# Gates of a query block applied tile by tile, and the gate bias as a fifth entry beside the experts' logits, in a two-layer graph and attention network on one core

## The reference: what is computed

```python
sx = jnp.einsum('bsh,ndh->bnsd', x, hl_w) + hl_b[None, :, None, :]
pad = sx == 0
q = jnp.einsum('bnsd,neod->bneso', sx, wq)
k = jnp.einsum('bnsd,nod->bnso', sx, wk)
v = jnp.einsum('bnsd,nod->bnso', sx, wv)
scores = jnp.einsum('bnesd,bntd->bnest', q, k) * d ** 0.5 + causal
att = jax.nn.softmax(scores, axis=-1)
qkv = jnp.einsum('bnest,bntd->bnesd', att, v)
qkv = jnp.where(pad[:, :, None], 0.0, qkv)
out = jnp.transpose(qkv, (0, 1, 3, 2, 4)).reshape(b, nh, s, ne * d)
gs = jax.nn.softmax(jnp.einsum('bnsf,nef->bnse', out, gate_w) + gate_b[None, :, None, :], axis=-1)
mixed = jnp.einsum('bnsed,bnse->bnsd', out.reshape(b, nh, s, ne, d), gs)
hn = layernorm(mixed + resid, ln_g, ln_b)
```

## Time and profile before

| | |
|---|---|
| median of 3 runs | 3369.95 us (3368.48 to 3369.95) |
| the profiled execution | 3364.28 us, span 3362.6 us |
| granted clock of TensorE, mean | 0.934 |
| PE matmuls | 2953.1 us busy, 88% |
| POOL | 1772.2 us, 53% |
| DVE | 1898.3 us, 56% |
| ACT | 1254.0 us, 37% |
| PE's row maxima L1736, held by DVE's reading L1906 | 91.4 us in 52 waits |

### The profile page before, as it was taken

The page is one execution under the profiler, slowest core; times in us unless marked ns, Lnnn a source line. Parts: engine busy times, 40 slices in busy tenths (PEclk is TensorE's granted clock), DMA queues, the critical chain, the costliest instruction groups (busy, mean ns, idle before and its releaser), DMA issues. The chain is left out here.

```text
span 3362.6 us, 45520 instructions
## 1 busy us (share of the span) xinstructions
PE 2953.1 (88%) x17338; PEld 1822.7 (54%) x17338; DVE 1898.3 (56%) x3632; ACT 1254.0 (37%) x1712; POOL 1772.2 (53%) x956
## 2 busy tenths in 40 slices
PE   7998987679997889899999999788988999999953
PEld 3467666468885455555555555455555554545532
DVE  3555764487733465665655651245656565565566
ACT  2232320355633233343434344323433443434433
POOL 0030020233220357778889899636687888888014
PEclk9999888889998899999999999888999999999976
DMA  9961100299970000000000000000000000000001
GB/s 391 423 246 41 63 1 8 87 290 282 268 130 18 1 1 1 1 1 1 1 1 1 1 4 1 1 1 1 1 1 1 1 1 1 1 1 1 1 8 36
DMA packets 63624, 195.20 MB, mean 58 GB/s; under 512 B 8244, under 2 KB 25010, under 8 KB 53427
## 3 DMA queue, kind: packets, MB, share of 16 engines
q1 hardware_dynamic: 38658, 147.98, 11.4%
q0 software_dynamic: 24752, 44.31, 7.3%
HBM read 188.86 MB, written 3.41 MB: 57 GB/s over the span
## 5 line engine op out<-in xcount | busy, mean ns | idle before, releaser
L2052 POOL TENSOR_TENSOR at_acc<-at_acc,at_pt 128x1024 f32<-128x1024 f32 (+3 forms) x674 | 1445.8, 2145 | 257.4 <-ACT at_pt L1843 178.0
L1843 ACT ACTIVATE at_pt<-at_psR 128x1024 f32<-128x1024 f32 (+3 forms) x776 | 697.8, 942 | 993.2 <-PE at_psR L1752 686.7
L1906 DVE TENSOR_REDUCE at_mx<-at_psR 128x2 f32<-128x1024 f32 x576 | 702.1, 1225 | 493.5 <-PE at_psR L1736 492.0
L1770 PE MATMUL at_psO<-at_pt,v 128*64 128x512 f32 (+3 forms) x3104 | 716.5, 584 | 2.1 <-DVE at_oT L1939 1.8
L1736 PE MATMUL at_psR<-at_khi,at_qhi 64*128 64x512 f32 (+3 forms) x1568 | 353.5, 447 | 134.4 <-DVE at_mx L1906 91.4
L1736 PEld LDWEIGHTS at_psR<-at_khi,at_qhi 64*128 64x128 f32 x1568 | 155.8, 189 | 411.8 <-issue 360.2
L1770 PEld LDWEIGHTS at_psO<-at_pt,v 128*64 128x64 f32 x3104 | 194.2, 140 | 339.6 <-issue 239.1
L1316 PE MATMUL ga_acc<-h,ga_ring 128*128 128x257 f32 (+1 forms) x1352 | 304.7, 385 | 31.0 <-ACT ga_ring L1210 27.3
L1749 PE MATMUL at_psR<-at_qhi,at_klo 64*128 64x512 f32 (+2 forms) x1552 | 307.8, 392 | 6.6 <-ACT at_pt L1843 5.7
L1316 PEld LDWEIGHTS ga_acc<-h,ga_ring 128*128 128x128 f32 (+1 forms) x1352 | 257.3, 192 | 76.6 <-ACT ga_ring L1210 36.0
L1749 PE MATMUL at_psR<-at_qlo,at_khi 64*128 64x512 f32 (+2 forms) x1552 | 294.7, 375 | 0.0
(11 more groups left out here) (335 smaller groups left out, 3531.3 us busy)
## 6 DMA issues: line engine op xcount, KB each, us to landing
gc_rows<-in_adj SPq DMA_DIRECT2D x26, 1664.0 KB, 17.4
ga_rows<-in_adj SPq DMA_DIRECT2D x26, 1664.0 KB, 9.9
ga_ring<-in_adjT POOLq DMA_DIRECT2D x78, 512.0 KB, 23.6
gc_cols<-in_adjT SPq DMA_DIRECT2D x26, 1024.0 KB, 14.9
gc_ring<-in_adjT SPq DMA_DIRECT2D x26, 512.0 KB, 8.2
gc_ring<-in_adjT SPq DMA_DIRECT2D x13, 256.0 KB, 2.8
ga_ring<-in_adjT POOLq DMA_DIRECT2D x13, 256.0 KB, 11.0
out_x<-X SPq DMA_DIRECT2D x6, 512.0 KB
```

The lines of the kernel that those rows point to most:

```text
L1770: ins = pe.matmul(columns(psO[lanes[l], :], g), v1[:, t, (2 * hp + l) * D:(2 * hp + l + 1) * D], packed(pt[:, g % PTS, l, 0:w], g), start= ...
L1843: act.activation(pt[:, g % PTS, :, 0:w], psR[:, slot_of["score", g] % SLOTS, :, 0:w], ACT.Exp).then_inc(e_ready, 1)
L1906: dve.tensor_reduce(mx[:, u % 2, :, s, c:c + 1].rearrange("p l o -> p (l o)"), got[:, :, 0:w], AX.X, ALU.max).then_inc(p1_read, 1)
L2052: pool.tensor_tensor(to, to, got, ALU.add).then_inc(added, 1)
```

## The change

`gate_pieces` keeps pieces 0 and 1 in their steps. Piece 2 is gone from it. In its place POOL weighs one tile of 128 queries per instruction (`weigh`), tiles 0 and 1 behind its adds of step 3, tiles 2 and 3 behind those of step 4. DVE sums the experts of one tile at a time (`sum_of_experts`) between the first and the second maxima of a step: in steps 5, 6, 7 and 8 counted from the start of unit e = 0 (in block 3 the last two are steps 0 and 1 of unit e = 1; in block 2 the steps are 4, then two tiles in step 0 and one in step 1 of unit e = 1). The tile's statistics follow behind the step's second maxima. Where a unit has fewer than five steps, all tiles are weighed, summed and measured in the step in which the pieces stood. ACT waits by tiles. The reduce writes into `scrap`, which the maxima's instructions use too, in place of `mixed`.

The gate bias is no longer added. `onx` has a fifth entry: ACT writes the biases of the half's two heads there (`gate_biases`, once per half), POOL writes ones as its denominators, and the reciprocal, the product and the sum of piece 0 run over five entries.

```diff
@@ -1534,12 +1534,38 @@
     if u and e == 0:
         hp, b, _ = UNITS[u - 1]
         if ls >= 5:
-            return [(hp, b, i) for i in range(3) if k == 2 + i]
-        return [(hp, b, i) for i in range(3 if ls == 1 else 1)] if k == ls - 1 else []
+            return [(hp, b, i) for i in range(2) if k == 2 + i]
+        return [(hp, b, i) for i in range(2 if ls == 1 else 1)] if k == ls - 1 else []
     if u > 1 and e == 1 and steps_of(u) == 3 and k == 0:
         hp, b, _ = UNITS[u - 2]
-        return [(hp, b, 1), (hp, b, 2)]
+        return [(hp, b, 1)]
     return []
+
+
+def block_weighed(u, k):
+
+    ls, e = steps_of(u), UNITS[u][2]
+    if u and e == 0:
+        hp, b, _ = UNITS[u - 1]
+        if ls >= 5:
+            return [(hp, b, s) for s in range(SUB) if k == 3 + s // 2]
+        return [(hp, b, s) for s in range(SUB)] if ls == 1 else []
+    if u > 1 and e == 1 and steps_of(u) == 3 and k == 0:
+        hp, b, _ = UNITS[u - 2]
+        return [(hp, b, s) for s in range(QBLOCKS[b][1] // P)]
+    return []
+
+
+SUM_STEPS = {5: (4, 5, 5, 6), 7: (5, 6, 7, 8)}
+
+
+def block_summed(u, k):
+
+    ls, e = steps_of(u), UNITS[u][2]
+    if not u or ls < 5 or e > 1:
+        return block_weighed(u, k)
+    hp, b, _ = UNITS[u - 1 - e]
+    return [(hp, b, s) for s in range(SUB) if SUM_STEPS.get(ls, (5, 6, 7, 8))[s] == k + e * ls]
 
 
 FIRST_TURNS = [("k", 0, 0), ("q", 0), ("q", 1), ("r", 0), ("k", 0, 1), ("q", 2)]
@@ -1606,20 +1632,19 @@
...
-        junk = m.sb("at_junk", [P, P])
+        scrap = m.sb("at_scrap", [P, P])
...
-        onx = m.sb("at_onx", [P, SUB, NE, 2 * NE + 2])
-        rden = m.sb("at_rden", [P, SUB, NE, 2])
-        gp = m.sb("at_gp", [P, SUB, NE, 2 * NE])
+        onx = m.sb("at_onx", [P, SUB, NE + 1, 2 * NE + 2])
+        rden = m.sb("at_rden", [P, SUB, NE + 1, 2])
+        gp = m.sb("at_gp", [P, SUB, NE + 1, 2 * NE])
...
-        mixed = m.sb("at_mixed", [P, SUB, P])
...
@@ -1826,7 +1855,9 @@
...
-                        act.wait_ge(mix_done, block_number(hp, b))
+                        last = block_number(hp, b) - 1
+                        seen = min(s0 + 2, QBLOCKS[last % NQB][1] // P) if EXPERTS[b] == 1 else SUB
+                        act.wait_ge(mix_done, tiles_upto(last // NQB, last % NQB) + seen)
...
@@ -1848,9 +1879,18 @@
...
+                        if b == NQB - 1 and hp + 1 < NPR:
+                            gate_biases(hp + 1)
+
+                def gate_biases(hp):
+                    both = gb_sb[:, 2 * hp:2 * hp + 2, :].rearrange("p l g -> p (l g)")
+                    act.activation(onx[:, :, NE, 0:2 * NE], both.unsqueeze(1).broadcast_to([P, SUB, 2 * NE]),
+                                   ACT.Copy).then_inc(bias_set, 1)
...
+                act.wait_ge(w_loaded, 64)
+                gate_biases(0)
...
@@ -1963,47 +2005,55 @@
...
+                        dve.wait_ge(bias_set, hp + 1)
...
-                                [P, ws * NE, 2, NE]), ALU.mult))
+                                [P, ws * (NE + 1), 2, NE]), ALU.mult))
...
-                        link(dve.tensor_tensor(gl[:, 0:ws, :], gl[:, 0:ws, :],
-                                               gb_sb[:, 2 * hp:2 * hp + 2, :].rearrange("p l g -> p (l g)").unsqueeze(
-                                                   1).broadcast_to([P, ws, 2 * NE]), ALU.add))
...
-                    elif piece == 1:
+                    else:
...
-                                          rden[:, 0:ws, :, :], ALU.mult).then_inc(gate_ready, 1)
-                    else:
-                        dve.wait_ge(weighed, at_block + 1)
-                        if at_block < NPR * NQB - 1:
-                            link(dve.tensor_reduce(mixed[:, 0:ws, :], on[:, 0:ws, :, :].rearrange("p s e c -> p s c e"),
-                                                   AX.X, ALU.add))
-                        else:
-                            link(dve.tensor_tensor(on[:, 0:ws, 0:2, :], on[:, 0:ws, 0:2, :], on[:, 0:ws, 2:4, :], ALU.add))
-                            link(dve.tensor_tensor(mixed[:, 0:ws, :], on[:, 0:ws, 0, :], on[:, 0:ws, 1, :], ALU.add))
-                        hsl = hn[:, c0 // P:c0 // P + ws, hp * P:(hp + 1) * P]
-                        dve.tensor_tensor(hsl, hsl, mixed[:, 0:ws, :], ALU.add).then_inc(mix_done, 1)
-                        dve.wait_ge(mix_done, at_block + 1)
-                        for s in range(ws):
-                            for l in range(2):
-                                ins = dve.bn_stats(hn_stats[:, s, l, :], hsl[:, s, l * D:(l + 1) * D])
-                        link(ins)
-                        for s in range(ws):
-                            for l in range(2):
-                                ins = dve.bn_aggr(hn_mv[:, c0 // P + s, 2 * hp + l, :], hn_stats[:, s, l, :])
-                        link(ins)
+                                          rden[:, 0:ws, 0:NE, :], ALU.mult).then_inc(gate_ready, 1)
+
+                def statistics(hp, tile, s):
+                    for l in range(2):
+                        ins = dve.bn_stats(hn_stats[:, s, l, :], hn[:, tile, hp * P + l * D:hp * P + (l + 1) * D])
+                    link(ins)
+                    for l in range(2):
+                        ins = dve.bn_aggr(hn_mv[:, tile, 2 * hp + l, :], hn_stats[:, s, l, :])
+                    return ins
+
+                def sum_of_experts(hp, b, s):
+                    tile, n = QBLOCKS[b][0] // P + s, tiles_upto(hp, b) + s + 1
+                    dve.wait_ge(weighed, n)
+                    dve.wait_ge(p1_read, pieces[0])
+                    link(dve.tensor_reduce(scrap[:, :], on[:, s, :, :].rearrange("p e c -> p c e"), AX.X, ALU.add))
+                    there = hn[:, tile, hp * P:(hp + 1) * P]
+                    dve.tensor_tensor(there, there, scrap[:, :], ALU.add).then_inc(mix_done, 1)
+                    dve.wait_ge(mix_done, n)
+
+                def last_sum():
+                    hp, b = NPR - 1, NQB - 1
+                    t0, n = QBLOCKS[b][0] // P, tiles_upto(NPR, 0)
+                    dve.wait_ge(weighed, n)
+                    link(dve.tensor_tensor(on[:, :, 0:2, :], on[:, :, 0:2, :], on[:, :, 2:4, :], ALU.add))
+                    link(dve.tensor_tensor(on[:, :, 0, :], on[:, :, 0, :], on[:, :, 1, :], ALU.add))
+                    there = hn[:, t0:t0 + SUB, hp * P:(hp + 1) * P]
+                    dve.tensor_tensor(there, there, on[:, :, 0, :], ALU.add).then_inc(mix_done, SUB)
+                    dve.wait_ge(mix_done, n)
+                    for s in range(SUB):
+                        link(statistics(hp, t0 + s, s))
...
@@ -2015,13 +2065,23 @@
                 queries(2)
                 for u in range(NU):
                     for k in range(steps_of(u)):
-                        for half in range(2):
-                            for piece in max_pieces(u, k, half):
-                                row_max(u + 2, *piece)
+                        for piece in max_pieces(u, k, 0):
+                            row_max(u + 2, *piece)
+                        summed = block_summed(u, k)
+                        if steps_of(u) >= 5:
+                            for x in summed:
+                                sum_of_experts(*x)
+                        for piece in max_pieces(u, k, 1):
+                            row_max(u + 2, *piece)
                         for x in late_turns(u, k):
                             turn(*x)
                         for x in gate_pieces(u, k):
                             gate(*x)
+                        if steps_of(u) < 5:
+                            for x in summed:
+                                sum_of_experts(*x)
+                        for hp, b, s in summed:
+                            link(statistics(hp, QBLOCKS[b][0] // P + s, s))
                         if u >= LAST_POOL:
                             add_up(FIRST[u] + 2 * k)
                             add_up(FIRST[u] + 2 * k + 1)
@@ -2033,8 +2093,8 @@
...
-                    [P, SUB * NE * 2, D]), ALU.mult).then_inc(weighed, 1)
-                gate(NPR - 1, NQB - 1, 2)
+                    [P, SUB * NE * 2, D]), ALU.mult).then_inc(weighed, SUB)
+                last_sum()
...
@@ -2051,18 +2111,17 @@
...
-                def gate(hp, b, piece):
-                    ws = QBLOCKS[b][1] // P
-                    if piece == 1:
-                        pool.wait_ge(gate_ready, block_number(hp, b) + 1)
-                        both = on[:, 0:ws, :, :].rearrange("p s e (l d) -> p (s e l) d", l=2)
-                        pool.tensor_tensor(both, both, wgt[:, 0:ws, :, :].rearrange("p s e l -> p (s e l)").unsqueeze(
-                            2).broadcast_to([P, ws * NE * 2, D]), ALU.mult).then_inc(weighed, 1)
+                def weigh(hp, b, s):
+                    pool.wait_ge(gate_ready, block_number(hp, b) + 1)
+                    both = on[:, s, :, :].rearrange("p e (l d) -> p (e l) d", l=2)
```

(18 more changed lines are left out.)

## The result

| | before | changed |
|---|---|---|
| median | 3369.22 us (3368.4 to 3369.95, 4 runs) | 3336.51 us (3332.14 to 3340.6, 4 runs) |
| profiled execution | 3364.28 us | 3340.60 us |
| span | 3362.6 us | 3338.9 us |

The ratio is 0.9907, interval 0.9893 to 0.9922: faster by 31 us, or 0.9%. The same kernel against the same one before on another chip gave 0.9928 (0.9911 to 0.9944), 24 us. The two profiled executions differ by 23.7 us, all of it in the attention stage. That is less than the medians' 32.7: the kernel before took 3369 us in this comparison and 3364 us in its profile and in every later comparison, and the profile of after is its slowest execution. So what follows explains 24 us; the rest of the first comparison isn't explained. Forecast were 45 us, 3325 in the range 3306 to 3356.

The account below looks back on a forecast made before the run. PE was taken to be held by DVE's late maxima, with POOL's chain capping the gain. 63.4 us gained, less 18 for tile sums and 0.6 for start and end, gave 45: 3325 us, range 3306 to 3356.

Parts of the forecast that it names:

- (1): Blocks 2 to 6: removing piece 2 in one go gains 10.4, 7.2, 6.5, 4.6, 3.0 us, POOL capping 3 to 6; 63.4 in all.
- rival B: POOL is the bound, only its idle rests go: 11 us or less, 3359 to 3370; chance 0.07.
- E: Rival: DVE's added waits near 0 or all covered, gain over 55 us, 3306 to 3315; chance 0.07.
- (2): Weighing in four costs 0.57 us more; PE's bias wait of 1.10 goes, so POOL gains 0.55 us a block.
- (4): Per-tile reduce, add and statistics on DVE between maxima hold PE 0.8 us a tile: 18 us back in all.
- w: The wait of a tile's add on DVE for POOL's running add, 0 to 2.4 us; PE is held w - 0.35.
- the cover: PE's spare time where POOL paces the steps: 0.7, 1.8, 3.1, 4.5 us in blocks 3 to 6, hiding tile costs.
- (5): Block 0's pieces in one step and the border of the halves: between -1.5 and +1.5 us, taken as 0.
- Rival A: The port takes most of the gain in each tile's add: gain 7 to 25 us, 3345 to 3363; 0.16 with another rival.
- C: Rival: tile adds lose the port more than once, waiting up to 4.9 us; slower, 3370 to 3400; chance 0.10.

Follow-up runs that it names:

- e9: Changed kernel with block 2's sums in four steps, one tile each, in place of two tiles in one step; 3326.65 us, 0.9886.
- e10: e8 with block 2's sums in four steps, one tile each; 3296.83 us, 0.9795 of the kernel before.
- e5: Changed kernel with all tiles weighed, summed and measured at once, as before, in units of fewer than five steps; 3334.18 us, 0.9912.
- e7: Changed kernel without DVE's add into hn: the reduce takes the residual as fifth entry, copied by ACT in unit e = 2; 3322.51 us, 0.9876.
- e11: e10 without the gate logits' shift by their maximum (maximum and subtraction left out); 3293.24 us, 0.9776 of the kernel before.
- e8: e7 with POOL's weighing one step later in units of 9 steps and more; 3306.78 us, 0.9828 of the kernel before.

## Why the prediction was right, and where it wasn't

- **(1), the caps, right.** The next unit starts four groups after POOL's add, in blocks 3 to 6 within 0.3 to 0.5 us of the forecast. POOL and PE as two chains, the later one deciding, is what the profile shows; rival B in its full form (POOL allows nothing) is out, E (over 55) too.
- **(2), too good by 0.3 to 0.5 us a block.** "With the bias add gone PE's wait of 1.10 goes" failed: it fell to 0.74 and POOL's wait for the weights from 4.68 to 4.23, since the DVE instruction behind it with two SBUF operands, the subtraction, took over the port's wait (1.57 us). The weighing by tiles was right (1.055).
- **(4), mis-sized for block 2.** 3.4 us for two tiles in a step: e9 took 5.9 us out of unit e = 1 in the first half and 2.9 in the second by spreading them. The waits alone were 2.9 us. What was missing is the clock: my text expected its low windows to vanish, and one came back behind two short waits. e10 shows the same without adds: one wait of 1.09 us and the clock behind it made 3.1 us. For single tiles w stayed within its bounds (0 to 2.0 in blocks 3 to 6, 0.7 on average over all adds, where I took 1.15), but PE's waits did not follow w - 0.35: behind the add with w of 1.9 us in block 3 they were 0.42 and 0.60 us, behind one with 0.4 in block 6 0.61.
- **(4), the cover, half right.** In blocks 4 to 6 PE's waits behind the tiles (up to 0.8 us) were covered, as the slack said. But the lead of the table's first columns shrank behind the first exponential of e = 1 all the same, by 1.5, 0.8 and 0.5 us. The only PE wait that grew there is one that I hadn't looked at: the queries' copy behind POOL-bound exponentials on ACT (`qlo`, 0.6 to 2.2 us once a block, 25.5 to 39.9 us in total). That it is the cause is argued, not tested. ("Were the cover gone everywhere it would be 16 in each half" is a slip: four blocks at 3.2 and block 2 at 5.0 make 17.8. Nothing else uses it.)
- **(5), wrong for block 1**: not 0, and outside its bounds of 1.5 either way, but +2.3 to +2.6 us in unit e = 1, 6 us in the sum over both halves, since the first tile's add met a POOL instruction at its start (2.33 us, where the add of both tiles took 0.60 before). e5 took it back. The border cost 0.8 as its bounds allowed.
- **Rival A** did not come: it wanted w near 2.4 each time, and it was 0.7 on average. The port's wait still costs: e7, without the adds, is 16 us faster. **C**, more than one lost turn, never: no add of the changed kernel was over 2.33 us.

The sum by blocks: 45, less 2 x 2.8 in block 2, 6 in block 1, 8.7 in blocks 3 to 6 and 0.8 at the border, is 24, as the profile has it. Of the 8.7, 3.2 are the caps of (2) and 2.6 the last block, 1.6 of it the clock; the rest fits the wait for `qlo`. All of these blocks missed in one direction; that the range held owes something to its width.

By the Trainium skill, SBUF — State Buffer, section Who interferes with whom, every VectorE instruction with two SBUF inputs meets GpSimd's reads, not a certain one. The trace agrees (0.19 us for the subtraction before, 1.25 after). Read so, the rule says where to look: which such instruction stands behind the bias add while POOL is at work. It doesn't say that the wait must move on, and in e11 it didn't.

## What to carry to other kernels

A wait for a shared port belongs to the moment, not to the instruction: take one instruction away and the next with two SBUF operands can inherit it, if it starts while POOL works (the subtraction did; the product, which starts in POOL's gap, took its 0.33 us; in e11 none inherited it in full). So look at such instructions in the stretch one by one, or give them a form with one operand, as the residual in the reduce does. When a long stall of one engine hides another engine's lag, work out both chains and expect the smaller gain; and a change that gave nothing by itself (weighing later) may give 0.5% on top of another (no add), as each had covered the other. Spread inserted work over steps so that each fits the slack of one. And price a short wait of PE with the clock that may fall behind it, not by its length alone: where it fell here, it added 1.5 us and more.

## What the runs showed of the hardware that wasn't expected

- Two PE waits of 1.62 and 1.28 us in block 2 were followed by a granted clock of 0.51 (1.2 GHz) for 7 us; with the same work spread over one more step it stayed at 1.00. In e8 one wait of 1.09 us there was followed by 0.52 for 3.5 us. Waits of 0.7 to 2.2 us in block 4 of the changed kernel left it at 1.00.
- The same wait of 2.17 us at the same place in the last block was followed by 0.54 for 3.5 us in one execution of the changed kernel and by 1.00 in another. That makes 1.6 us; units of one kernel that differ by 1.5 us (53.0 and 54.5 in block 5) differ in this. What decides it isn't shown.
- A 128x128 add on DVE took from 0.29 to 2.33 us, by where POOL was in its instruction of about 2.4 us; it never waited for a second one.
- A reduce of four strided rows of 128 took 1.07 us, of five 1.30: adding an entry costs 0.23 us, a separate add 0.99.
